# Attention of a five-stage audio tower: scores of four row groups at once, transposes back into their banks, values as column strips, tokens two pairs ahead

## What is computed

```python
# h = tokens(x): [16, 128, 256]
x = jnp.einsum('btki,oik->bto', xb, conv_w) + conv_b
x = x + xb.mean(axis=2)                       # then a LayerNorm with gamma and beta
# attention, 16 heads of 16 channels, on LayerNorm(h); layer 0 sees the 64 latest keys, layer 1 all earlier keys
scores = q @ k.T / 4 (masked); attn = softmax(scores); out = attn @ v
h = h + out @ W_out
# mixture of experts: layer 0 has 16 experts (2 a token) and a shared MLP, layer 1 has 64 experts (3 a token)
```

## Time and profile before

| What | Value |
|---|---|
| time, median of 3 runs | 1459.58 us (1443.99 to 1460.77) |
| profiled execution, its own time | 1452.52 us |
| its span | 1450.8 us |
| mean granted clock of TensorE | 0.943 |
| PE busy | 1314.3 us, 91% of the span |
| ACT / DVE / POOL busy | 565.7 / 532.5 / 360.2 us (39 / 37 / 25%) |
| stages in the trace, us | start to 33, attention of layer 0 to 346, its experts to 636, attention of layer 1 to 942, its experts to the end |

### The profile page before, as it was taken

How to read it: one execution, slowest core, us unless ns; L and a number is a source line. 1 busy time by engine, 2 the same in 40 slices (tenths; PEclk the granted TensorE clock), 3 DMA queues, 4 the chain that set the end, 5 groups by cost and what they waited for, 6 DMA issues and landing times.

```text
span 1450.8 us, 25791 instructions
## 1 busy us (share of the span) xinstructions
PE 1314.3 (91%) x7680; PEld 1105.3 (76%) x7680; DVE 532.5 (37%) x2676; ACT 565.7 (39%) x1960; POOL 360.2 (25%) x343
## 2 busy tenths in 40 slices
PE   5899999986888898879999998199999999999996
PEld 4677777773577677547778777199999999999995
DVE  4356566542234443332555555212211221222121
ACT  1666666651122222135666665033223223322331
POOL 3123333212035444400122222312112212221221
PEclk8899999987999899999999999599999999999998
DMA  9700000001156556351000000269999999999993
GB/s 332 295 16 30 29 29 29 15 12 40 63 121 144 130 113 144 69 191 68 16 24 9 8 7 7 84 221 304 306 312 310 303 305 317 304 304 309 315 297 78
DMA packets 148816, 218.04 MB, mean 150 GB/s; under 512 B 9604, under 2 KB 117094, under 8 KB 148737
## 3 DMA queue, kind: packets, MB, share of 16 engines
q1 hardware_dynamic: 129824, 197.18, 40.1%
q0 software_dynamic: 18944, 20.28, 8.3%
HBM read 178.51 MB, written 45.19 MB: 154 GB/s over the span
## 4 chain that ended last, share of the span: by engine, by line
PE 75%; issue 6%; DVE 6%; ACT 4%; DMA 4%; POOL 3%; POOLq 0%; DVEq 0%; SPq 0%; ACTq 0%
PE bank L1104 16%; PE bank L1117 15%; PE bank L817 9%; PE bank L842 6%; PE bank L827 4%; PE bank L795 4%; PE bank L998 3%; PE bank L1044 3%; ACT probs L1188 2%; PE bank L887 2%; DMA stream<-arena,slot_token 2%; PE bank L776 2%; PE bank L1119 2%; PE bank L1008 2%; PE bank L803 1%
## 5 line engine op out<-in xcount | busy, mean ns | idle before, releaser
L1343 ACT ACTIVATE dhidT<-bank,b1T 128x128 f32<-128x128 f32 x512 | 145.9, 368 | 335.9 <-PE bank L1104 335.9
L1104 PE MATMUL bank<-probsT,arena 128*128 128x128 f32 x2048 | 241.4, 277 | 0.1
L1104 PEld LDWEIGHTS bank<-probsT,arena 128*128 128x128 f32 x2048 | 236.0, 193 | 0.5 <-DVE probsT L1751 0.5
L1117 PE MATMUL bank<-arena,dhidT 128*128 128x256 f32 x1024 | 231.6, 379 | 0.0
L1117 PEld LDWEIGHTS bank<-arena,dhidT 128*128 128x128 f32 x1024 | 189.8, 190 | 23.2
L1188 ACT ACTIVATE probs<-probs,neg_max 128x128 f32<-128x128 f32 x512 | 197.9, 390 | 10.4 <-DVE neg_max L1443 10.1
L720 POOL DMA_INDIRECT stream<-probsT,slot_token x64 | 98.9, 1545 | 402.9 <-DMA stream<-probsT,slot_token 352.8
L1772 DVE TENSOR_SCALAR probsT<-bank,slot_gate 128x256 f32<-128x256 f32 x64 | 30.9, 483 | 384.9 <-PE bank L1119 378.9
L1443 DVE CUSTOM_DVE_ANT_0 probs<-bank,mask 128x128 f32<-128x128 f32 x512 | 117.4, 286 | 124.9 <-PE bank L817 122.3
L817 PE MATMUL bank<-kT,qT 32*128 32x256 f32 x512 | 146.9, 412 | 4.5 <-DVE neg_max L1443 2.1
L634 POOL DMA_INDIRECT rows<-ffn_in,scatter_i x80 | 79.8, 998 | 259.4 <-DVE scatter_i L1565 207.2
(11 more groups left out here) (172 smaller groups left out, 1719.8 us busy)
## 6 DMA issues: line engine op xcount, KB each, us to landing
arena<-L_ffn_w SPq DMA_DIRECT2D x128, 1024.0 KB, 7.4
rows<-zeros SPq DMA_DIRECT2D x13, 1024.0 KB, 13.1
drows<-rows SPq DMA_DIRECT2D x64, 132.0 KB, 7.7
arena<-L_ffn_w_gate SPq DMA_DIRECT2D x16, 352.0 KB
arena<-L_ffn_w_up SPq DMA_DIRECT2D x16, 352.0 KB
early<-rows SPq DMA_DIRECT2D x16, 264.0 KB, 2.7
early<-x SPq DMA_DIRECT2D x8, 512.0 KB
arena<-L_ffn_w_down SPq DMA_DIRECT2D x16, 256.0 KB
```

Source lines behind the costliest of these rows:

```text
L1104: mm = pe.matmul(bank[2 + 2 * (u % 2) + half][:, jj * P:(jj + 1) * P], w1_sb[u][:, c, j * P:(j + 1) * P], drowsT[:, u % 2, c, :], start=c ...
L1117: pe.matmul(bank[6 + u % 2][:, 0:D], dhidT[:, u % 2, j, :], w2_sb[u][:, j, :], start=j == 0, stop=False)
L1343: last_ = act.activation(dhidT[:, u % 2, j, :], bank[2 + 2 * (u % 2) + half][:, jj * P:(jj + 1) * P], ACT.Gelu, bias=b1T[:, j, bass.ds(e, 1)])
```

## The change

- **Scores.** `scores(L, i, t)` writes all four row groups into four banks: for each `m`, the four `b` one behind the other. The score banks are now banks 0 to 3. One semaphore step announces all of them.
- **Transposes.** `turn_probs` writes into the score bank that its heads came from, so banks 2 and 3 no longer belong to transposes. The scores of the next half wait until all four banks of this half have been copied (`turned`).
- **Values.** `v_pad` replaces `v_wide`: a head's stationary operand has 32 columns, in which its 16 channels stand left or right. Each `b` writes its own 32 partitions of `mix_bank`; `values(L, i, t)` issues the 16 heads in one call, the four strips in turn.
- **Tokens.** The mean of the two rows goes into the convolution weights (half of the identity is added to them at the start), so `sum_x` and a DVE pass go. In layer 0, tokens are made two pairs ahead: body `i` holds `turn_x(i + 2)` and `conv(i + 2)`, and the tokens of pairs 0 and 1 come before the loop. The load of pair 1 moves ahead of the router's weights; the loads of pairs 2 and up stay behind the zero fills.
- **Order.** The bodies of PE, ACT, DVE and POOL are rewritten, and `front_order` and `back_order` number the jobs of the front and back banks in their new order. In it `turn_inverse(i)` comes at the end of body `i`, `count(i - 2)` and `spread_inverse(i - 1)` follow at the start of the next one, and `place(i - 2)` comes behind all four `greatest(i, 0, b)`.

The diff, cut to its core (bodies with their removed lines left out):

```diff
-        score_bank, turn_bank, mix_bank = bank[0:2], bank[2:4], bank[4]
+        score_bank, mix_bank = bank[0:4], bank[4]
...
+        X0, X1, CONV0, CONV1, TURN, Q, K, V = 0, 1, 2, 3, 4, 5, 6, 7
+        tokens = lambda i: [(i, X0), (i, X1), (i, CONV0), (i, CONV1)]
+        def front_order(L):
+            order = tokens(0) if L.n == 0 else []
+            order += [(0, TURN), (0, Q), (0, K)]
+            order += tokens(1) if L.n == 0 else []
+            for i in range(PAIRS):
+                ahead = L.n == 0 and i + 2 < PAIRS
+                order += [(i, V)]
+                if ahead:
+                    order += [(i + 2, X0), (i + 2, X1)]
+                if i + 1 < PAIRS:
+                    order += [(i + 1, TURN)] + ([(i + 2, CONV0), (i + 2, CONV1)] if ahead else []) + [(i + 1, Q), (i + 1, K)]
+            return {job: n for n, job in enumerate(order)}
+        INVERSE, SPREAD, OUT, TURN_FFN, ROUTE, COUNT = range(6)
+        def back_order():
+            order = [(0, INVERSE)]
+            for i in range(1, PAIRS + 2):
+                for p, k in ((i - 2, COUNT), (i - 1, SPREAD), (i - 1, OUT), (i - 1, TURN_FFN), (i - 1, ROUTE), (i, INVERSE)):
+                    if 0 <= p < PAIRS:
+                        order += [(p, k)]
+            return {job: n for n, job in enumerate(order)}
...
+            load_x(1, False)
...
-            load_x(1, False)
             sp.wait_ge(const_p, 3)
             fill_zeros()
-            with sp.Fori(2, PAIRS) as i:
+            for i in range(2, 4):
+                load_x(i, False)
+            with sp.Fori(4, PAIRS) as i:
                 load_x(i, False)
...
-            def scores(L, i, t, b):
-                if t == 0 and b == 0:
...
-                wait(pe, L.max_done, 8 * i + 4 * t + b - 1)
-                row = 32 * b
+                wait(pe, L.turned, 8 * i + 4 * t)
                 for m in range(DC):
-                    last = pe.matmul(score_bank[b % 2][:, 2 * m * P:2 * (m + 1) * P], qT[row:row + 32, m, t, :],
-                                     kT[row:row + 32, m, t, :, :], start=True, stop=True)
+                    for b in range(SBANKS):
+                        row = 32 * b
+                        last = pe.matmul(score_bank[b][:, 2 * m * P:2 * (m + 1) * P], qT[row:row + 32, m, t, :],
+                                         kT[row:row + 32, m, t, :, :], start=True, stop=True)
             def turn_probs(L, i, t, b):
-                n = 8 * i + 4 * t + b
-                wait(pe, L.exp_done, n + 1)
-                wait(pe, L.turned, n - 1)
+                wait(pe, L.exp_done, 8 * i + 4 * t + b + 1)
                 for j in range(HEADS_PER_BANK):
-                    last = pe.transpose(turn_bank[b % 2][:, j * P:(j + 1) * P], probs[:, t, head(b, j), :], ident[:, :])
+                    last = pe.transpose(score_bank[b][:, j * P:(j + 1) * P], probs[:, t, head(b, j), :], ident[:, :])
-            def values(L, i, t, b):
-                wait(pe, L.turned, 8 * i + 4 * t + b + 1)
-                if b == 0:
-                    fb, fn = front(L, i, L.KF + 3)
-                    wait(pe, L.front_free[fb], fn + 1)
-                    wait(pe, L.mix_done, i)
+            def values(L, i, t):
+                wait(pe, L.turned, 8 * i + 4 * t + SBANKS)
+                fb, fn = front(L, i, V)
+                wait(pe, L.front_free[fb], fn + 1)
+                wait(pe, L.mix_done, i)
                 for j in range(HEADS_PER_BANK):
-                    m, own = divmod(head(b, j), P // HD)
+                    m, r = divmod(j, 2)
                     col = (2 * m + t) * P
-                    last = pe.matmul(mix_bank[:, col:col + P], v_wide[:, DC * t + m, own * P:(own + 1) * P],
-                                     probsT[:, b, j * P:(j + 1) * P], start=b == 0 and j == 0,
-                                     stop=b == SBANKS - 1 and j % 2 == 1, skip_group_check=True)
+                    for b in range(SBANKS):
+                        own = 2 * b + r
+                        last = pe.matmul(mix_bank[b * STRIP:(b + 1) * STRIP, col:col + P],
+                                         v_pad[:, DC * t + m, own * STRIP:(own + 1) * STRIP], probsT[:, b, j * P:(j + 1) * P],
+                                         start=j == 0, stop=r == 1, skip_group_check=True)
...
+                    ahead = L is L0 and there(i + 2, PAIRS)
+                    if now:
+                        scores(L, i, 0)
                     if before_:
+                        values(L, i - 1, 1)
+                    if there(i - 2, PAIRS):
+                        count(L, i - 2)
                     if before_:
                         spread_inverse(L, i - 1)
+                    if now:
+                        project_v(L, i)
+                        turn_probs(L, i, 0, 0)
+                    if ahead:
+                        turn_x(i + 2)
+                    if now:
+                        turn_probs(L, i, 0, 1)
                     if before_:
                         project_out(L, i - 1)
                     if now:
+                        turn_probs(L, i, 0, 2)
+                        turn_probs(L, i, 0, 3)
+                        scores(L, i, 1)
+                        values(L, i, 0)
+                    if next_:
+                        turn_normed(L, i + 1)
+                    if now:
+                        turn_probs(L, i, 1, 0)
+                    if ahead:
+                        conv(i + 2)
+                    if next_:
+                        project_qk(L, i + 1, 0)
+                    if now:
+                        turn_probs(L, i, 1, 1)
+                    if next_:
+                        project_qk(L, i + 1, 1)
+                    if now:
+                        turn_probs(L, i, 1, 2)
                     if before_:
+                        turn_ffn_in(L, i - 1)
                         route(L, i - 1)
+                    if now:
+                        turn_probs(L, i, 1, 3)
+                        turn_inverse(L, i)
...
+                    ahead = L is L0 and there(i + 2, PAIRS)
+                    if now:
+                        exponentials(L, i, 0, 0)
+                    if there(i - 2, PAIRS) and L is L1:
+                        router_exp(L1, i - 2)
                     if before_:
                         keep_spread(L, i - 1)
                     if now:
+                        exponentials(L, i, 0, 1)
+                        keep_turned(L, i, 0, 0)
+                        keep_v(L, i)
+                        exponentials(L, i, 0, 2)
+                        keep_turned(L, i, 0, 1)
+                        exponentials(L, i, 0, 3)
+                        keep_turned(L, i, 0, 2)
+                        keep_turned(L, i, 0, 3)
+                    if ahead:
+                        keep_xT(i + 2)
+                    if now:
+                        exponentials(L, i, 1, 0)
+                    if next_:
+                        keep_normedT(L, i + 1)
+                    if now:
+                        exponentials(L, i, 1, 1)
+                        keep_turned(L, i, 1, 0)
+                        exponentials(L, i, 1, 2)
+                    if next_:
+                        keep_q(L, i + 1)
+                    if now:
+                        exponentials(L, i, 1, 3)
+                        keep_turned(L, i, 1, 1)
+                    if next_:
+                        keep_k(L, i + 1)
+                    if now:
+                        keep_turned(L, i, 1, 2)
+                    if before_:
+                        keep_ffn_inT(L, i - 1)
+                    if now:
+                        keep_turned(L, i, 1, 3)
+                        keep_inverse(L, i)
                     if before_ and L is L0:
                         router_exp(L0, i - 1)
                         keep_for_shared(i - 1)
...
+                    own = conv_wT[:, 2 * k + c, c * P:(c + 1) * P]
+                    last = dve.scalar_tensor_tensor(out=own, in0=ident[:, :], scalar=0.5, in1=own, op0=ALU.mult, op1=ALU.add)
+            last.then_inc(conv_ready, 1)
...
-                    dve.scalar_tensor_tensor(out=tok[:, t, :], in0=x_sum[:, t, :], scalar=0.5, in1=front_bank[b][:, 0:D],
-                                             op0=ALU.mult, op1=ALU.add).then_inc(L0.front_free[b], 1)
+                    dve.tensor_tensor(tok[:, t, :], front_bank[b][:, 0:D], conv_b[:, :], ALU.add).then_inc(L0.front_free[b], 1)
...
+                    ahead = L is L0 and there(i + 2, PAIRS)
                     if now:
                         greatest(L, i, 0, 0)
                     if there(i - 2, PAIRS) and L is L1:
                         less_greatest(i - 2)
                     if now:
+                        for b in range(1, SBANKS):
+                            greatest(L, i, 0, b)
+                    if next_ and L is L0:
+                        front_c(i + 1)
+                    if next_ and L is L1:
```

(14 more changed lines are left out.)

301 lines of the change are left out of this document (106 added, 195 removed).

## The result

The changed kernel took 1494.2 us (median of 4 runs, 1492.39 to 1495.76), the kernel before 1458.17 us on the same chip (4 runs, 1443.99 to 1460.77): ratio 1.026, 95% interval 1.022 to 1.030, slower. The profiled execution took 1492.95 us (span 1491.2, mean granted clock 0.876; before 1452.52, 1450.8, 0.943). PE's busy time fell from 1314.3 to 1199.8 us.

What follows compares the result with a forecast made beforehand. PE's work was taken to bound attention before the change. Against the 1450.8 us span, start +23, layer 0 +4 and layer 1 +13 gave +40, about +42 with loop waits: span 1493, time 1495 us, range 1436 to 1545.

Steps and rivals of the forecast that it cites:

- PE's work: Attention pairs: scores 1.2 us and values 1.1 a half, 11.8 us less a pair; 23.7 left in layer 0, 19.2 in layer 1.
- The chain in its place: Attention pairs: waits between engines through place, spread and choose set periods of 36.4 us in layer 0, 33.0 in layer 1.
- the walk: Adding up one attention pair step by step through the engines at whole clock: 36.4 us in layer 0, 33.0 in layer 1.
- Rival 3: Attention: PE's work stays the bound, engines overlap over pairs; periods about 29 and 26 us, 1368 in all; chance 0.10.
- The start: Before pair 1's scores: PE waits for pair 2's load behind the zero fills; cost +23 us.
- Layer 0 after the start: Layer 0 attention: first step 33 us, five of 36.4, tail -3, clock +15; +4 us in all.
- Layer 1, seven steps: Layer 1 attention: 242 us before; then 220 at whole clock plus 35 for the clock, 255, so +13.
- the +2 for waiting steps in the loops: Loops: extra steps of waiting, unseen in the profile, raise the total from +40 to about +42 us.
- The clock: Attention: idle PE drops to 1.2 GHz in every pair; +2.5 us a pair in layer 0, +5 in layer 1.
- the upper end of its range: Attention: transposes not counting as activity keep the whole first half at 1.2 GHz; some +4 us more a pair, 60 in all.
- Rival 1: Attention: clock stays whole because PE works denser between gaps; 1443 us, no difference; chance 0.22.
- rival 4: Attention: PE stays at 1.2 GHz for most of it, its work becoming 47 and 38 us; 1550 to 1650; chance 0.06.

Runs made afterwards that it cites:

- three moves: Changed kernel with pair 2's load ahead of the zero fills, spread_inverse ahead of count, and turn_ffn_in and route a step earlier: 1406.6 us.
- the strips with and without filler: Kernel before with only v_pad and column strips, one values call a half: 1520.6 us; with eight useless blocks ahead of each call: 1456.3 us.
- the 16 shown: Changed kernel with twelve useless 128 x 128 blocks between count and spread_inverse, where PE stood idle: 1478.0 us, 16 less.
- with filler, the three-move kernel: Kernel with three moves, plus useless multiplications in PE's remaining waits in both layers: 1406.75 us.
- the wide values: Kernel with three moves, but values with v_wide's 128 columns, bank after bank in one call a half, instead of column strips: 1424.1 us.

## Why the prediction held, point by point

1495 was forecast and 1494.2 measured. The mechanism that was named is what the runs show: PE's work shrinks as costed, the chain through `place`, spread and `choose` takes its place, the start waits for a load, and the clock falls. That the number came out within 1 us is luck: layer 1 was measured from a wrong base and forecast too long, and these two errors cancel.

- **PE's work** fell as costed: scores 1.15 us (1.2), values 1.08 (1.1). The gain of 2.38 that the Trainium skill gives for three strips ("TensorE: Matmul & The Clock Gate", Part 3), by which the prediction estimated 1.7 us, is not borne out for four strips in turn.
- **The chain in its place** is shown, not only argued: the wait for the count's copy is 5.35 us (5), 54.8 in all, and taking it away by order alone won 38 us, a higher clock included. DVE took pair 2's scores 2.9 us late (33.5 against 36.4 in the walk). Rival 3 (1368) fell with pairs of 38; its kind of kernel needed three moves to come to 1406.6.
- **The start**: +21.6 against +23, confirmed by the load moved alone (20.8 earlier).
- **Layer 0 after the start**: -2.1 against +4. Five pairs took 38.4 on the mean (38.9 forecast); the step from pair 1 to 2 took 29.0, where 33 and the clock were expected. With the load early it did take 33.0: behind the long wait the body was 4 us shorter, which the sum did not see. That DVE, POOL and ACT had finished ahead in it is the likely reason.
- **Layer 1, seven steps**: the step of the sum that failed. The prediction read 242 us for them off the third row, 643 to 885. PE's timeline of before shows whose scores stand there:

```profile
866.13 1.95 PE L803 MATMUL bank<-w_qkv,normedT 128*128 128x256 f32 x8
868.40 1.10 PE L817 MATMUL bank<-kT,qT 32*128 32x256 f32 x4 [0.32 <-issue]
...
882.06 3.33 PE L887 MATMUL bank<-w_out,mixedT 128*128 128x256 f32 x8 [1.48 <-DVE mixedT L1459]
885.32 1.44 PE L817 MATMUL bank<-kT,qT 32*128 32x256 f32 x4
```

  Pair 7's first scores are those at 868.40, behind its projection of V; at 885.32, behind `project_out`, its second half begins. So 242 us are seven steps and a half; seven took 225.5. Against this the forecast of 255 was +29.5, not +13, and with it the sum comes to 1511. Measured were 238.7, +13.2. The middle steps were near (36.9 against 38), the first two took 54.3 where 65 with their clock price were forecast: the walk's 26 and 29 were right (25.7 and 28.6), the 5 us of clock in each did not come.
- **Layer 1's tail**, from pair 7's first scores to the experts' first transposes, took 73.2 us before (868.40 to 941.61) and 75.5 now (907.69 to 983.17). The sum had nothing for its +2.3.
- **What else helped the number**: experts of layer 0 and 1 differ by 6.9 and -1.2 us between the two executions and were put at nothing, and the +2 for waiting steps in the loops rests on no row. The stretches that the change touches add to +34.7, where +40 was forecast.
- **The clock**: 0.83 and 0.79 in the two attentions, in the 0.7 to 0.85 forecast. That waits can cost more than their length is shown best by the strips with and without filler, 64 us apart. The reason that the prediction gave for the upper end of its range, a first half wholly at 1.2 GHz, did not come: in pair 2 the clock is whole again from about 130 us, within the first half, and `project_out` takes 1.89 us at 132.66. Rival 1 (1443, clock whole) fell, rival 4 (1550 and up) too: conv and the projections of Q and K kept the whole clock (379 and 380 ns an instruction over five pairs of layer 0). The trace agrees with the rule that the throttled clock is the default and activity releases it (the Trainium skill, "TensorE: Matmul & The Clock Gate", Part 1): 20 us without work at the start stand at 0.50. Its price was forecast too high, 50 us (15 and 35); the walk leaves some 29 to it. How much of these is the clock's remains open beyond the 16 shown: with filler, the three-move kernel's pairs in layer 1 were 31.0 us at a clock of 0.98 and not 28.5, so there the walk is some 2.5 us a pair too short for other reasons, which no run settles. With the wide values it was too long (30.6 measured, 32.0 forecast). It found the largest wait, but its steps are not good to 2 us a pair.

## What to carry to other kernels

Before taking work off an engine that is 95% busy, walk the chain that would be next, in the order in which the new program will stand. Here the walk put it 0.7 us a pair below PE's work in layer 0 and above it in layer 1, so 11.8 us less work could win next to nothing, and the clock and a late load made a loss of it. The fix was not more overlap of matmuls but three moves of what stands ahead of what: with the same matmuls, pairs of layer 0 fell from 38.4 to 32.3 us. A small result that holds the only bank of its kind must not be queued ahead of a step that another engine waits for. Idle time of PE can cost more than its length: with two waits of 2 us a pair and less work, the strips alone took 43.2 us a pair where 37.0 had been. But a higher clock is not always worth its price: in the three-move kernel filler raised it to 0.97 and 0.98 in the two attentions and won nothing. And when a stretch is to be compared, name the instruction at each end: 16.5 us of this forecast were half a pair counted as part of seven.

## What the hardware showed that was not expected

- Less work made the kernel 63 us slower (1520.6), and eight useless 128 x 128 blocks a half made it 64 us faster again (1456.3), with the granted clock of most of layer 0's attention at 0.80 and 0.96 (68.1 to 325.3 and to 320.0).
- Four row groups ran side by side (16 instructions in 1.15 to 1.17 us, as long as one bank's four) in whichever order the program wrote them. Four column strips did so nearly in full when issued in turn, 1.08 us for 32 instructions, and in part when issued bank by bank, 2.46; with 128 columns they take 3.84.
